# First batch's rows gathered and normed tile by tile, one gather per quad, and buffers cleared elsewhere

## The reference

```
# mixture ("moe0", 32 experts, 4 per token)
y   = sum_k weight[token, k] * expert_{idx[token, k]}(x[token])
x   = x + y                               # 4 rows to gather and add for each token
# rotary attention (16 heads of 16), and sinks attention (32 query heads of 64, 8 key heads)
xn  = (x - mean(x)) / sqrt(var(x) + eps)
q, k, v = split(xn @ W);  q, k = rope(q), rope(k)
p   = softmax(mask(q @ k.T) * scale)      # sinks: one more column, the head's sink s, in the sum
x   = x + (p @ v) @ W_out
```

## Time and profile before

| | |
|---|---|
| median of three runs | 3999.8 us |
| profiled execution, its own time | 3998.9 us |
| its span, first to last instruction | 3996.8 us |
| busy over the span | PE 83%, DVE 70%, ACT 58%, POOL 45% |
| mean granted TensorE clock | 0.895 of full |
| rotary, from its first gather to the end of its units | 840 to 1327 us |
| sinks, from its first load to the end of its products | 1609 to 2894 us |

### The profile page before, as it was taken

The page is one execution under the profiler, slowest core; times in us unless marked ns, Lnnn a source line. Parts: engine busy times, 40 slices in busy tenths (PEclk is TensorE's granted clock), DMA queues, the critical chain, the costliest instruction groups (busy, mean ns, idle before and its releaser), DMA issues. The chain is left out here.

```text
span 3996.8 us, 68531 instructions
## 1 busy us (share of the span) xinstructions
PE 3298.8 (83%) x19706; PEld 2600.3 (65%) x19707; DVE 2798.3 (70%) x6275; ACT 2301.6 (58%) x5976; POOL 1778.6 (45%) x3039
## 2 busy tenths in 40 slices
PE   7799976947888489499899899999846499999574
PEld 3355555736667377378778778778745288888453
DVE  5599966747777666578588678768573388888742
ACT  3599933427777344488588678778512266666221
POOL 0299933568664044465266266355337300000165
PEclk9699987979999689799999999999957699999666
DMA  2011133440000336210010010000064400000535
GB/s 87 17 48 48 50 125 99 139 92 25 22 9 1 150 110 135 89 33 19 12 34 20 12 30 24 13 13 19 15 191 67 112 1 1 1 1 1 164 72 112
DMA packets 139454, 221.36 MB, mean 55 GB/s; under 512 B 28912, under 2 KB 114800, under 8 KB 137408
## 3 DMA queue, kind: packets, MB, share of 16 engines
q1 hardware_dynamic: 108432, 156.23, 12.0%
q0 software_dynamic: 30720, 61.44, 7.7%
HBM read 162.60 MB, written 54.80 MB: 54 GB/s over the span
## 5 line engine op out<-in xcount | busy, mean ns | idle before, releaser
L1271 POOL DMA_INDIRECT ex_xr<-scratch_rows,mo_token x288 | 286.8, 996 | 323.8 <-PE bank L1330 162.4
L598 POOL TENSOR_TENSOR sc_h<-sc_h,sc_c 128x512 f32<-128x512 f32 x256 | 326.9, 1291 | 198.0 <-DVE sc_h L635 189.9
L3125 DVE TENSOR_TENSOR sa_pT<-bank,sa_pT 128x512 fp32r<-128x512 f32 x512 | 330.0, 686 | 39.2 <-ACT sa_pT L2982 29.5
L2974 ACT ACTIVATE sa_p<-bank,sa_nm 128x512 f32<-128x512 f32 x512 | 347.8, 692 | 1.8 <-DVE sa_nm L3116 1.4
L635 DVE TENSOR_TENSOR_SCAN sc_h<-sc_da,bank 128x512 f32<-128x512 f32 x256 | 311.1, 1220 | 38.2 <-ACT sc_da L578 23.4
L2799 PE MATMUL bank<-sa_kT,sa_qT 128*128 128x512 f32 x1024 | 336.1, 439 | 1.5 <-DVE residual L3079 1.5
L2823 PE MATMUL bank<-sa_pT,sa_v 128*128 128x256 f32 x2048 | 309.1, 294 | 28.1 <-DVE sa_pT L3125 26.9
L3112 DVE TENSOR_REDUCE sa_mx<-bank 128x2 f32<-128x1024 f32 x256 | 312.0, 1219 | 26.9 <-PE bank L2801 23.0
L1348 PE MATMUL bank<-mo_w_gu,ex_xT 128*128 (+2 forms) x1152 | 308.7, 395 | 1.3 <-issue 0.7
L2823 PEld LDWEIGHTS bank<-sa_pT,sa_v 128*128 128x128 f32 x2048 | 262.7, 192 | 53.6 <-DVE sa_pT L3125 40.3
L1396 ACT ACTIVATE ex_xT<-bank 128x256 f32<-128x256 f32 (+1 forms) x288 | 105.4, 366 | 307.0 <-PE bank L1330 286.2
(11 more groups left out here) (403 smaller groups left out, 9530.1 us busy)
## 6 DMA issues: line engine op xcount, KB each, us to landing
scratch_ys<-ex_yo SPq DMA_DIRECT2D x192, 128.0 KB, 2.3
mo_w_gu<-in_w_gu SPq DMA_DIRECT2D x2, 9216.0 KB, 26.9
sc_c<-scratch_c SPq DMA_DIRECT2D x64, 256.0 KB, 3.1
sa_share<-scratch_shares SPq DMA_DIRECT2D x256, 64.0 KB, 2.6
mo_w_dn<-in_w_dn SPq DMA_DIRECT2D x2, 4608.0 KB, 46.7
scratch_rows<-ln_stage SPq DMA_DIRECT2D x64, 128.0 KB, 1.9
mo_w_dn<-in_w_dn SPq DMA_DIRECT2D x2, 4096.0 KB, 35.3
ex_xr<-scratch_rows,mo_token POOLq DMA_INDIRECT x288, 2.8
```

What stands on the lines that cost most here:

```text
L598: pool.tensor_tensor(h, h, C[u], ALU.mult).then_inc(used.sem, 1)
L1271: pool.indirect_dma_start(xr[u][:, :], None, rows, bass.IndirectOffsetOnAxis(ap=token[:, i:i + 1], axis=0), bounds_check=rows.shape[0] - 1 ...
L2974: act.activation(pr[h][:, :], SC[2 * s_ + h][:, :], ACT.Exp, bias=nm[:, col:col + 1], scale=SCALE, accum_out=rs[:, col:col + 1]).then_inc( ...
L3125: dve.tensor_tensor(spot(1), PT[h][:, :].rearrange("p (k n) -> p k n", k=TPB), spot(0).bitcast(F32), ALU.subtract).then_inc(*inc("kept_d"))
```

## The change

What it does, by place:

- `Combine.place` gives the four experts of tile 0, then those of tile 1, and so on; an add waits for the add before it in the same tile. Statistics are taken by tile (`tile_stats`), moments by single steps (`moment`); ACT's root waits for 6 of the 7 steps.
- Rotary, start: POOL issues all 16 gathers of batch 0 first. The 8 memsets of `qT` and those of `v` 0 and 1 go to DVE; `v` 2 and 3 stay on POOL, behind `put_group(0, (0, 1))`, and the first 8 gathers of batch 1 behind them. DVE, ACT and PE go through batch 0 tile by tile: adds, statistics, norm, turn, and the first group's projection.
- Rotary, loop: the next batch's statistics one tile in each of the units 0 to 3, all moments in unit 4, the root in unit 5.
- Sinks, start: tile by tile as well; the low part of WQ is taken by POOL, behind the gathers and the mask; ACT copies WQ's high part between the tiles 1 and 2; PE takes `keys_values` of the tiles 0 and 1 as soon as these are there, through a bank (`OB`) that is shared by all turned tiles.
- Sinks, loop: one gather behind `total` of each quad of the groups 0 to 3. The next batch's statistics go one per quad into group 6, the moments one per step into group 7, the root behind step 7.

```
     def place(self, m):
-        b, r = divmod(m, self.PER)
-        k, i = divmod(r, TPB)
-        return b * TPB + i, (b * TPB + i) * M0_K + k
+        return m // M0_K, m
...
 rotary, POOL
-                for m in range(8):
+                for m in range(PER):
                     merge.fetch(pool, m)
...
-                for u in range(2):
-                    for hh in range(HG):
...
-                        pool.memset(qT[u][rows, hh * SEQ:(hh + 1) * SEQ].bitcast(F32), 0.0).then_inc(*inc("made"))
-                for u in range(4):
-                    pool.memset(vv[u][:, :].bitcast(F32), 0.0).then_inc(*inc("made"))
-                for m in range(8, PER + PER // 2):
-                    merge.fetch(pool, m)
...
                 put_group(0, (0, 1))
                 pool.sem_inc(sig["qput"].sem, 2)
+                for u in range(2, 4):
+                    pool.memset(vv[u][:, :].bitcast(F32), 0.0).then_inc(*inc("made"))
+                for m in range(PER, PER + PER // 2):
+                    merge.fetch(pool, m)
                 put_group(1, range(TPB))
...
 rotary, DVE
+                for u in range(2):
+                    dve.memset(vv[u][:, :].bitcast(F32), 0.0).then_inc(*inc("blank_v"))
                 for i in range(TPB):
+                    for k in range(M0_K):
+                        merge.add(dve, i * M0_K + k)
+                    stats(i)
+                    dve.wait_ge(*at("stat", i + 1))
+                    moments(i, 1)
+                    invert(i, 1, i + 1)
                     stand(0, i)
+                    if i == 0:
...
+                                dve.memset(qT[u][rows, hh * SEQ:(hh + 1) * SEQ].bitcast(F32), 0.0) \
+                                   .then_inc(*inc("blank_q"))
+                    else:
+                        low_v(0, i - 1)
...
 sinks, SP
-                sp.wait_ge(*at("wlow", 3))
+                sp.wait_ge(*at("wq_low", 1))
 sinks, POOL
+                pool.wait_ge(*at("whigh", 3))
+                pool.tensor_tensor(WQ[1][:, :], raw_q, WQ[0][:, :].bitcast(F32), ALU.subtract).then_inc(*inc("wq_low"))
...
                     def steps(g, first, last):
-                        if g < 4 and b + 1 < BATCH:
-                            if b and first:
-                                pool.wait_ge(*at("outp", b * TPB))
-                            for r in range(4):
-                                merge.fetch(pool, (b + 1) * PER + g * 4 + r)
+                        if first and 1 <= b < BATCH - 1:
+                            pool.wait_ge(*at("outp", b * TPB))
...
                             sink_minus_max(q, g, qt)
                             total(q, qt)
+                            if g < 4 and b + 1 < BATCH:
+                                merge.fetch(pool, (b + 1) * PER + g * QUADS + qt)
...
 sinks, PE, first batch
-                        pe.wait_ge(*at("made", 5))
-                        for i in range(TPB):
-                            turn_x(b, i)
-                        pe.wait_ge(*at("wlow", 3))
+                        turn_x(0, 0)
+                        pe.wait_ge(*at("wlow", 2))
+                        keys_values(0, 0)
+                        turn_x(0, 1)
+                        keys_values(0, 1)
+                        turn_x(0, 2)
+                        turn_x(0, 3)
...
+                        if b == 0 and i == 1:
+                            pe.wait_ge(*at("wq_low", 1))
+                            pe.wait_ge(*at("made", 5))
                         if i == 1:
                             project(first_q, 0, 0)
...
 sinks, ACT
-                root(0)
                 for i in range(TPB):
+                    if i == 2:
+                        act.wait_ge(*at("wq_in", 16))
+                        act.activation(WQ[0][:, :], raw_q, ACT.Copy).then_inc(*inc("whigh"))
+                    root(i, 1, i * 8 + 6)
                     high_x(0, i)
...
-                            if last and p == STEPS_ - 2 and b + 1 < BATCH:
-                                root(b + 1)
+                            if last and p == STEPS_ - 1 and b + 1 < BATCH:
+                                root((b + 1) * TPB, TPB, TPB * 8 + b * 8 + 6)
...
 sinks, DVE
+                for i in range(TPB):
+                    for k in range(M0_K):
+                        merge.add(dve, i * M0_K + k)
+                    stats(i)
+                    dve.wait_ge(*at("stat", i + 1))
+                    moments(i, 1)
+                    invert_root(i, 1, i + 1)
+                    stand(0, i)
+                    if i == 0:
                         low_w(0, raw_k, WK)
                         low_w(1, raw_v, WV)
-                    if m == 10:
-                        low_w(2, raw_q, WQ)
...
                     low_x(0, i)
...
+                            if g == G - 2 and s_ == 1 and b + 1 < BATCH:
+                                stats((b + 1) * TPB + qt)
+                            if last and p < 7 and b + 1 < BATCH:
+                                if p == 0:
+                                    dve.wait_ge(*at("stat", (b + 2) * TPB))
+                                moments((b + 1) * TPB, TPB, (p,))
```

More of the change, by code:

```diff
@@ L1139, in counted, with tile_stats, moment @@
             fetched.counted(16 * (TILES * M0_K // self.RING))
-def batch_stats(c, dve, b, bn, stat):
-    for i in range(TPB):
[L1146 to L1162, removed]
+def tile_stats(c, dve, i, bn, stat):
+    dve.bn_stats(bn[:, i % TPB * 6:(i % TPB + 1) * 6], c.x[:, i * D_MODEL:(i + 1) * D_MODEL]).then_inc(stat.sem, 1)
+def moment(st, step, first, n, bn, mean, var, tmp):
+    dve, cut = st.eng, slice(first, first + n)
+    bnv = bn[:, first % TPB * 6:(first % TPB + n) * 6].rearrange("p (t s) -> p t s", s=6)
+    if step == 0:
+        st.then(dve.tensor_tensor(mean[:, cut], bnv[:, :, 1], bnv[:, :, 4], ALU.add))
+    if step == 1:
+        st.then(dve.tensor_tensor(tmp[:, cut], bnv[:, :, 1], bnv[:, :, 4], ALU.subtract))
+    if step == 2:
+        st.then(dve.tensor_tensor(var[:, cut], bnv[:, :, 2], bnv[:, :, 5], ALU.add))
+    if step == 3:
+        st.then(dve.tensor_tensor(tmp[:, cut], tmp[:, cut], tmp[:, cut], ALU.mult))
+    if step == 4:
+        st.then(dve.tensor_scalar(var[:, cut], var[:, cut], 1.0 / D_MODEL, LN_EPS, ALU.mult, ALU.add))
+    if step == 5:
+        st.then(dve.scalar_tensor_tensor(out=var[:, cut], in0=tmp[:, cut], scalar=0.25, in1=var[:, cut],
+                                         op0=ALU.mult, op1=ALU.add))
+    if step == 6:
+        st.then(dve.tensor_scalar(mean[:, cut], mean[:, cut], 0.5, None, ALU.mult))
 def remap_gate(c, gold, o2n, gate, bias, loads, loaded):
@@ L2419, in _, with stats, moments, invert @@
                 st = Steps(dve, sig["own"])
[L2420 to L2428, removed]
+                def stats(i):
+                    dve.wait_ge(*merge.tile_added(i))
+                    tile_stats(c, dve, i, bn, sig["stat"])
+                def moments(first, n, steps=range(7)):
+                    for step in steps:
+                        moment(st, step, first, n, bn, mean, var, tmp)
+                def invert(first, n, roots):
+                    cut = slice(first, first + n)
+                    dve.wait_ge(*at("root", roots))
                     st.then(dve.reciprocal(rstd[:, cut], tmp[:, cut]))
@@ L2538, in rotary @@
         for n, v in dict(
-                loaded=16 * len(LOADS), made=4 + 2 * HG + 4, own=8 * BATCH + 8, dput=2, qkept=2 * NG, stat=TILES, root=BATCH, stood=TILES, xturned=TILES,
+                loaded=16 * len(LOADS), made=6, blank_q=2 * HG, blank_v=2, own=8 * (TPB + BATCH - 1) + 8, dput=2,
+                qkept=2 * NG, stat=TILES, root=TPB + BATCH - 1, stood=TILES, xturned=TILES,
                 xkept=TILES, qp=NG * TPB, qraw=NG * TPB, vput=NG * TPB, klow=NG * TPB, own_q=(NG * TPB - 2) * 4,
@@ L2562, in sinks @@
         sig = {n: counter(c, "at_" + n) for n in (
[L2563 removed]
+            "loaded", "wq_in", "wo_in", "made", "whigh", "wlow", "wq_low",
             "xlow", "kvp", "kput", "own_k", "kturned", "kkept", "vput", "klow",
@@ L3033, in _, with stats, moments, invert_root @@
                 st = Steps(dve, sig["own"])
-                def stats(b):
-                    batch_stats(c, dve, b, bn, sig["stat"])
-                def moments(b):
-                    batch_moments(st, b, bn, mean, var, tmp)
-                def invert_root(b):
-                    cut = slice(b * TPB, (b + 1) * TPB)
-                    dve.wait_ge(*at("root", b + 1))
+                def stats(i):
+                    dve.wait_ge(*merge.tile_added(i))
+                    tile_stats(c, dve, i, bn, sig["stat"])
+                def moments(first, n, steps=range(7)):
+                    for step in steps:
+                        moment(st, step, first, n, bn, mean, var, tmp)
+                def invert_root(first, n, roots):
+                    cut = slice(first, first + n)
+                    dve.wait_ge(*at("root", roots))
```

(3 more changed lines are left out.)

134 lines of the change are left out of this document (61 added, 73 removed).

## The result

The changed kernel takes 3965.3 us (median of 4 runs, 3959.5 to 3967.0) against 4002.7 for the kernel before on the same chip (4 runs, 3999.4 to 4008.0): ratio 0.9904, 95% interval 0.9892 to 0.9917, or 37 us less. The profiled execution after took 3966.96 us, with a span of 3964.9 us: 31.9 us less than the span before.

What follows compares the result with a forecast made beforehand. Bounds: late gathers and POOL's queue at rotary's start, DVE's key chain at sinks' start, waits for POOL in sinks' loop. From 3998.9 us, -30 - 9 + 2 - 1 = -38 gave 3961, range 3946 to 3980.

Steps and rivals of the forecast that it cites:

- Gathers one per quad: Sinks' loop: spreading each group's block of four gathers removes ACT's and PE's waits for POOL; 30 us faster.
- the cover: Sinks' loop: POOL may be 2.4 us later before ACT waits; one gather takes 1.6, leaving 0.8 us.
- Rival (c): Sinks' loop: the gather per quad is on the path, slower from 0.8 us uncovered a quad; 4038 us, chance 0.05.
- (b): DVE memsets and adds hold POOL's gathers, rotary gains 4.5; sinks' quads lose cover, gain 26; 3969 us, chance 0.12.
- Rotary's start: Start of rotary: POOL's queue loses memsets and a wait, so both later puts end earlier; 9.0 us faster.
- (d): Tile order does nothing, POOL as late as before, only sinks' loop gains; 3971 us, chance 0.07.
- rotary's loop is 0, within 1: Loop of rotary: same instructions one unit later, so no change in time, within 1 us.
- 4.5 (memsets on DVE hold the gathers): Start of rotary, low end of the gain: DVE's memsets hold POOL's gathers up while they run; 4.5 us.
- Sinks' start: Start of sinks: POOL's 9.0 us WQ subtraction holds DVE, and PE restarts at 1.2 GHz; 2 us slower, 1 to 4.
- the second one I had worked out: Start of sinks: the subtraction catches tile 2's last moments, 2.7 us more, keys at 1655.7 instead of 1653.0.
- Rival (a): Start of sinks: POOL's subtraction does not hold DVE, or ends before tile 3; part 7 us faster, 3952 us, chance 0.15.
- Group 7: Sinks' group 7: root behind step 7, statistics and moments in DVE's gaps; 1 us faster for three batches, ends 0 and 4.

Runs made afterwards that it cites:

- pairs: The changed kernel with two gathers behind every second quad instead of one behind each: 3960.7 us, ratio 0.9900 to the kernel before.
- rotary_only: The kernel before with the changed rotary layer; of the sinks edits only the row order: 3989.9 us, ratio 0.9967 to the kernel before.
- split: The changed kernel with POOL's WQ subtraction written as 8 pieces of 128x512: 3960.2 us, ratio 0.9897 to the kernel before.
- memsets: The changed kernel with the clearing of `v` 2 and 3 moved from POOL to DVE too: 3955.0 us, ratio 0.9890 to the kernel before.
- both: The changed kernel with WQ's subtraction in 8 pieces and all `v` clearings on DVE: 3954.5 us, ratio 0.9885 to the kernel before.
- whole: The changed kernel itself, unaltered, run again beside variants of it: 3962.5 us, ratio 0.9908 to the kernel before.

## Why the prediction was right, by its own steps

The mechanisms held in the three large parts. That the sum came out within a microsecond is in part luck: the loop of sinks gave 1.6 us more than forecast and the loop of rotary some 3 that were put at nothing, while the start of rotary gave 1.2 us less, the start of sinks cost 1.6 more and group 7 gave 1.2 less in this profile.

*Gathers one per quad, 30 forecast:* 31.6 in the trace, 28.6 alone on the chip. The sum took batch 2's 10.1 us three times; the batches gave 11.9, 9.9 and 9.8. The forecast that the 1.6 us would go into `total`'s wait held as worked out (1.1 to 1.3 us of waiting left, "about 1"). What was mis-sized is the cover. The step "so POOL may be 2.4 us later before ACT waits" is true, but ACT's first waits are not yet time: `pairs` puts POOL 2.9 us late, ACT waits 0.4, and under 0.1 is lost. Rival (c), slower from 0.8 us uncovered a quad, was further away than I put it, and (b)'s loss of cover did not happen.

*Rotary's start, 9.0 forecast:* the two puts came out at 901.33 and 929.21 against 901.2 and 929.2 (0.4 and 0.3 us later than forecast, counted from the first gather). POOL as the one late queue, and what is not in it any more, gave the number; (d) falls. The stand of "some 10 us" was 9.28. DVE had its last row at 867.7 and its last norm at 870.7, where I had 864 and at worst 870, and it cost nothing, as POOL was later. Two things around it failed. "Even with a colder clock it reaches the second in time" holds (it stood 4.01 us), but behind that second stand PE runs at the 1.2 GHz level:

```profile
929.00:935.00 6.00, 5.68 (x26) 5.08 (x27) 4.20 (x11) 2.25 (x6) 5.26 (x17) 0.50 0.00 0
```

In a row of windows the third number from the end is the granted clock, here 0.50 (ahead of it the busy time of each engine, behind it DMA's). Before, it was 0.66 in the five us behind that stand. The first group's last row comes 101.8 us behind the first gather, 109.5 before: 7.8 of the 9.0 arrive (batch 2's statistics lie in this stretch too, so not all of the 7.8 need be POOL's). And "rotary's loop is 0, within 1" was wrong: it gave 1.2 to 1.7 us at each of two changes of batch, where DVE's statistics and moments had stood in one block each ahead of the row-maxima. 7.8 and 3.2 make 11.0, where `rotary_only` measured 11.9. The profiled execution gave 3.0 of it back at its last products. Of the ends I had set, 4.5 (memsets on DVE hold the gathers) is refuted: gathers beside the 1.87 us memset take their usual 1.00 us.
"VectorE: DVE Perf Modes" of the Trainium skill, section "Zero memsets can be issued as uint32 (trn2)", had led me to an estimate of 2.3 us for each. The trace agrees: a row reads 1.87 us, but 0.40 us of idle time ("issue") stands ahead of it, and the second starts 2.28 us behind the first.

*Sinks' start, +2 forecast, ends 1 to 4:* +3.6 in the trace, +5.1 alone on the chip (interval 2 to 10). The sign and the mechanism held: a subtraction of 9.0 us forecast, 8.80 measured, and DVE held for 8.70. The case was the second one I had worked out, with tile 2's moments caught, keys at 1655.7 against 1653.65: +2.05 there, +2.6 measured. PE's part, put at some 1.5 us, was 1.0. The value of 2 mixed it with the milder case. Rival (a), no hold, is refuted by this row and by `split`.
The page "SBUF — State Buffer" of the Trainium skill, section "Who interferes with whom", is borne out at a length no row before had; 1.19 us in `split` shows that it is settled instruction by instruction.

*Group 7, -1 forecast:* +0.2 over three batches in this profile, and no run has this part alone. The four quads of group 7 did get shorter, in batch 2 from 7.43, 8.94, 8.23 and 6.82 us to 8.09, 7.07, 7.48 and 7.55, 1.2 less. From the last of them to the next first score it is 61.95, 61.34 and 60.60 us, where it was 59.8 to 60.2. Two things are in that. The norm starts 1.2 us later, as I had named and not priced: `memsets` has 60.55 three times, 0.4 to 0.8 more than before. And in the two long ones the granted clock was 0.94, in 60.60 and in those of `memsets` and before 0.97. In `split`, `memsets` and `both`, whose loop of sinks is the same, the stretch from group 4's second quad to the next first score is 2.1 us shorter over three batches than before, in `whole` 0.2 shorter. So the -1 lies inside what executions of like kernels show.

## What to carry to other kernels

Before pricing an edit at a start, list what the one late queue still has to issue, and subtract only what leaves that queue: it gave both puts to 0.4 us, while score 0 came 16 us earlier for nothing. A long elementwise instruction moved to an idle GpSimd is not off VectorE's path if both read SBUF with two operands; write it in pieces (2.6 us here, no better than leaving it on VectorE), or put it where VectorE rests. And a block of small jobs in a loop is best spread only until it fits the slack: two per place cost within 0.1 us of one here.

## What the runs showed of the hardware

- A 128x1 VectorE addition took 8.70 us while GpSimd subtracted 128x4096, and 1.18 us beside a 128x512 piece, instead of 0.16.
- VectorE's clearing of 128x2176 floats reads 1.87 us in its row, but two in a row start 2.28 us apart (0.40 idle ahead of each), and those of 64x512 read 0.48 and start 0.65 apart. GpSimd needs 1.87 (7.46 for four) and 0.57 (4.55 for eight), so it is the faster one here. Its gathers beside a VectorE clearing keep their 1.00 us.
- TensorE's granted clock at two short places differed from one kernel to the next. The last eight products of rotary took 1.97 us at full clock or 3.75 at the 1.2 GHz level; that is worth 3.0 us of span. The first block of output products of sinks took 7.17 us, or 10.01 with a granted clock of 0.72, the one and the other in two executions of the same kernel; `split` had the 10.01 too. The profiles of all three kernels with the old rotary ended it at full clock, five of the seven with the new one did not. Whether the shift in time causes that stays open.
